# Local attention: which signals TensorE awaits before it turns the queries

## The reference

```python
h = shift_token(x)
q, k, v = jnp.split(h @ wqkv, 3, axis=-1)      # 8 heads of 64 columns
q = l2norm(q) * qs
k = l2norm(k) * ksc
q, k = rotary_xpos(q, k)
o = local_attention(q, k, v)                   # windows of 64, each sees itself and the one before
x = x + o @ wo
...
h = a * jax.nn.gelu(g, approximate=False)      # feed-forward
x = x + h @ w2 + b2
```

## Time and profile before

| | us |
|---|---|
| median of 3 runs | 2104.4 (2103.34 to 2105.58) |
| time of the profiled execution | 2106.7 |
| its span, first to last instruction | 2104.9 |
| local attention, layer 0 | about 1300 to 1600 |
| feed-forward part of layer 0 | about 1600 to 1700 |
| local attention, layer 1 | about 1700 to 1980 |
| feed-forward part of layer 1 | about 1980 to 2105 |

### The profile page before, as it was taken

How to read it: one execution, slowest core, us unless ns; L and a number is a source line. 1 busy time by engine, 2 the same in 40 slices (tenths; PEclk the granted TensorE clock), 3 DMA queues, 4 the chain that set the end, 5 groups by cost and what they waited for, 6 DMA issues and landing times. The chain is left out here.

```text
span 2104.9 us, 38118 instructions
## 1 busy us (share of the span) xinstructions
PE 1719.8 (82%) x13216; PEld 959.9 (46%) x13216; DVE 1545.4 (73%) x3211; ACT 1215.5 (58%) x2673; POOL 931.1 (44%) x771
## 2 busy tenths in 40 slices
PE   5889888874899999885991575799998989999884
PEld 2333333332344444442440442566665656666553
DVE  5999999997477777751216475788885778888675
ACT  5778777762244444432444333788885368888621
POOL 5778777783002222222443133555552145555310
PEclk7999999998699999986996787999999999999897
DMA  4433343320311111101514423010000000000010
GB/s 147 123 111 107 115 125 107 106 65 16 106 26 39 41 37 42 42 20 45 147 56 130 140 84 116 11 26 18 17 17 18 19 11 22 22 17 17 19 41 23
DMA packets 107405, 125.56 MB, mean 60 GB/s; under 512 B 28804, under 2 KB 79151, under 8 KB 106224
## 3 DMA queue, kind: packets, MB, share of 16 engines
q1 hardware_dynamic: 103120, 115.07, 19.3%
q0 software_dynamic: 4096, 8.06, 1.2%
HBM read 71.60 MB, written 38.11 MB: 52 GB/s over the span
## 5 line engine op out<-in xcount | busy, mean ns | idle before, releaser
L394 POOL TENSOR_TENSOR m_bu<-m_dtu,m_brow 128x1024 f32<-128x1024 f32 x128 | 299.6, 2356 | 54.6 <-DVE m_hs L818 54.1
L818 DVE TENSOR_TENSOR_SCAN m_hs<-m_ps_da,m_bu 128x1024 f32<-128x1024 f32 x128 | 291.9, 2280 | 6.0 <-POOL m_bu L394 5.5
L1363 ACT ACTIVATE a_pt<-a_ps_s 128x1024 f32<-128x1024 f32 x128 | 131.0, 1024 | 225.6 <-PE a_ps_s L1141 225.6
L523 PE MATMUL m_ps_y_ps<-m_prod,m_ident 128*128 128x512 f32 x512 | 243.4, 598 | 0.0
L2913 ACT ACTIVATE l_pe<-l_ps_s,l_nbias,l_qs 128x128 f32<-128x128 f32 x512 | 226.4, 467 | 15.7 <-DVE l_nbias L3063 15.7
L1480 DVE TENSOR_REDUCE a_mpad<-a_ps_s 128x4 f32<-128x1024 f32 x128 | 156.8, 1225 | 91.6 <-PE a_ps_s L1133 90.5
L1133 PE MATMUL a_ps_s<-a_heads 32*128 32x256 f32 x1024 | 186.7, 444 | 43.5 <-DVE a_mpad L1480 29.0
L670 ACT ACTIVATE m_ps_da<-m_dt,m_a_neg 128x510 f32<-128x510 f32 x256 | 166.0, 681 | 73.1 <-DVE m_hs L818 72.4
L1141 PE MATMUL a_ps_s<-a_qm,a_heads 32*128 32x256 f32 x1024 | 184.3, 437 | 1.6 <-ACT a_pt L1363 1.2
L1067 POOL TENSOR_TENSOR a_rstd<-a_ve,a_mhalf 128x2 f32<-128x2 f32 x48 | 33.8, 705 | 301.5 <-DVE a_ve L1438 162.5
L828 DVE TENSOR_TENSOR m_prod<-m_hs,m_ps_c_ps 128x1024 f32<-128x1024 f32 x128 | 153.2, 1197 | 12.3 <-PE m_ps_c_ps L509 12.3
(11 more groups left out here) (344 smaller groups left out, 4210.6 us busy)
## 6 DMA issues: line engine op xcount, KB each, us to landing
m_brow<-state_rows SPq DMA_DIRECT2D x64, 512.0 KB, 4.3
slots<-m_void SPq DMA_DIRECT2D x16, 516.0 KB, 5.4
l_near<-l_v SPq DMA_DIRECT2D x64, 128.0 KB, 2.3
e_xs<-slots SPq DMA_DIRECT2D x16, 258.0 KB, 2.8
ys<-m_void SPq DMA_DIRECT2D x8, 512.0 KB, 5.4
qk<-a_qk SPq DMA_DIRECT2D x16, 256.0 KB, 2.0
a_heads<-qk SPq DMA_DIRECT2D x64, 64.0 KB
ew_w<-in_w SPq DMA_DIRECT2D x2, 2048.0 KB, 11.9
```

Source lines behind the costliest of these rows:

```text
L394: nc.gpsimd.tensor_tensor(bu[s % 4][:, :, :], dtu[p][:, :, :], b2, ALU.mult).then_inc(bu_rd, 1)
L523: last = pe.matmul(y_ps[:, h, :], ident[:, :], prod[d % 3][:, h, :], start=False, stop=(s == NS - 1))
L818: dve.tensor_tensor_scan(hs[s % 4][:, :, :].rearrange("p h t -> p (h t)"), da[s % 2][:, :, :, :].rearrange("p h q t -> p (h q t)"), bu[s % ...
L1363: nc.scalar.activation(pt[t % 2][:, :, :], s2[:, :, :], ACT.Exp).then_inc(exp_rd, 1)
```

## The change

`turn_q` keeps its wait for ScalarE's square of the projection only for chunks with i < kept[Q], the first two of a layer. For the other 30 chunks of each layer it no longer waits for it. Its other waits stay as they are, and no other instruction is added, removed or moved.

```diff
                 def turn_q(n, b, c):
                     l, i = at[n], NCH * b + c
                     pe.wait_ge(l.sum_rd[Q], i + 1)
-                    pe.wait_ge(l.sq_rd[Q], i + 1)
+                    if i < kept[Q]:
+                        pe.wait_ge(l.sq_rd[Q], i + 1)
                     at_least(pe, l.xT_sb[Q], i)
                     at_least(pe, l.pT_sb, NU * (i - 2))
                     for j in range(NP):
```

## The result

| | before | changed |
|---|---|---|
| median of the runs, us | 2103.96 (2103.34 to 2105.58, 4 runs) | 2080.03 (2079.15 to 2082.28, 4 runs) |
| ratio, 95% interval | | 0.988 (0.9868 to 0.9892) |
| profiled execution: time, span | 2106.7, 2104.9 | 2079.59, 2077.8 |

The change makes the kernel 23.9 us faster. The forecast was 26 us and 2078.5 us, with 2073 to 2088 as the range.

The account below looks back on a forecast made before the run. The bound was a closed ring from scores through maxima, exponentials, copy, `weigh` and `turn_q`, PE's list beside it, both holding the idle time. 58 x 0.43 + 0.98 + 0.35 = 26.3 us off 2104.4 gave 2078.1, rounded to 2078.5; range 2073 to 2088.

Parts of the forecast that it names:

- What `turn_q` waited for: PE's 22.8 us idle ahead of `turn_q` in 60 chunks was read as waiting for ACT's square of the queries.
- The ring: Local attention's closed chain scores, maxima, exponentials, copy, `weigh`, `turn_q`, scores: 8.96 us a turn, 8.53 after.
- The size of a step's gain: `turn_q` starting earlier in each of 58 steps was to save 0.43 us a step.
- low end: PE's idle time ahead of `turn_q`, mean 0.36 us, as the smaller gain a step; 22.2 us in all.
- like pair: `turn_k` behind the first `weigh`, 0.61 or 0.59 us after its start, taken as how closely `turn_q` would follow the second.
- The first steps: Each layer's first step, with no `weigh` ahead of `turn_q`: gains of 0.98 us in layer 0, 0.35 in layer 1.
- The sum: 58 x 0.43 + 0.98 + 0.35 = 26.3 us off the median of 2104.4 us: 2078.1, rounded to 2078.5.
- the four candidates: What might be late next: DVE, ACT, the turned keys' copy, POOL's sum; all keep room, the least 0.23 us on ACT.
- The held VectorE: Rival: DVE's long instruction returns every step, +0.66 us, leaving 7.8 us of gain: 2096.6 us; chance 0.06.
- PE's queue: Rival: after a blocking `weigh` wait, 0.17 us of gap stays ahead of `turn_q`, gain 16 us: 2088 us; chance 0.06.
- No effect: Rival: the idle time ahead of `turn_q` belongs to PE itself, so nothing changes: 2104 us; chance 0.04.
- The clock: Rival: PE without rest in the stage loses granted clock; at 0.90, 31 us slower: 2135 us; chance 0.02.

Follow-up runs that it names:

- E3: Kernel before with ACT's two squares exchanged, keys first, so the queries' square ends later; wait kept: 2170.55 us, 1.0137 of the kernel before.
- E2: Kernel before with ACT squaring the queries ahead of the copy of the turned keys, all waits kept: 2119.21 us, 0.9888 of the kernel before.
- E1: Kernel before with the wait dropped in layer 1 alone, layer 0 keeping it: 2128.2 us, 0.9937 of the kernel before.
- E5: Changed kernel with an early-satisfied wait for DVE's rotary products of the queries in place of the dropped one: 2110.43 us, 0.988 of the kernel before.
- E8: Changed kernel without the last of eight exponentials in each chunk but a layer's first: 2116.23 us, 0.9861 of the kernel before.
- E9: Changed kernel projecting only half of the values from block 1 on: 2119.4 us, 0.9873 of the kernel before.
- E7: Changed kernel with one more reduction of the key squares on DVE in each step: 2118.35 us, 0.9906 of the kernel before.
- E11: Changed kernel as it is, run again on another chip: 2082.37 us, 0.9881 of the kernel before.

## Why the prediction was right

**What `turn_q` waited for.** Right. The profile had called it "issue", and the prediction read it as ACT's square by the 0.10 us behind its end. E3 moved that end by 0.49 us and the idle time followed; E2 moved it the other way and the idle time vanished.

**The ring.** Right. The stalls added up, and none of it was given back. E1 shows it by halves and E3 as a slope: 0.49 us later in each step, 0.50 us more a step. The turn that was forecast at 8.53 us takes 8.54.

**The size of a step's gain.** Forecast 0.43 us, with 0.36 as the low end; measured 0.40 us: 29 steady steps went from 258.05 to 246.42 us in layer 0 and from 258.04 to 246.34 in layer 1, 23.3 us in all. The start of `turn_q` moved exactly as the like pair said, 0.59 and 0.61 us behind the start of `weigh`. What the term left out is what follows. Held up, `turn_q` was followed by the scores 0.99 us after its start; not held up, by 1407.04 - 1406.02 = 1.02 us, the second of its four transposes coming 0.16 instead of 0.14 us behind the first. 58 x 0.03 = 1.7 us of the 26.3 us: the term was sized too large by that.

**The first steps.** Forecast 0.98 and 0.35 us. From first to second maxima they went from 8.32 and 8.32 us to 7.36 and 7.45 us, so 0.96 and 0.87 us. The second was undersized, and part of what came was luck. VectorE's little idle time there, 0.35 us, came of its being late, and it was late because it had waited for the projections. PE and DVE in the kernel before:

```profile
1702.02 2.94 PE L2630 MATMUL l_ps_qk<-t_wqkv,l_hT 128*128 128x512 f32 x4
...
1704.13 0.69 DVE L3031 TENSOR_TENSOR l_c<-l_ps_qk,t_tab 128x512 f32<-128x512 f32 x1 [0.57 <-PE l_ps_qk L2630]
```

And the same projections in the changed kernel:

```profile
1688.11 2.49 PE L2630 MATMUL l_ps_qk<-t_wqkv,l_hT 128*128 128x512 f32 x4
```

In the steady steps the four take 1.88 us. How much of the longer time falls to them depends on when PE's clock rises there, and I had read it from one execution as if it were fixed. From 1702 to 1704 the granted clock of the kernel before was 0.51, from 1688 to 1690 that of the changed kernel 0.71. As long as `turn_q` waits for the square the length of the projections doesn't show: 8.32, 8.33 and 8.32 us with projections of 1.98, 2.50 and 2.94 us (before, layer 0; E1, layer 0; before, layer 1). Without that wait the step follows them: 7.36 us with 1.98, 7.45 with 2.49, 7.75 with 2.85 (E5, layer 0) and 7.89 with 3.05 (E8, layer 1). So with the 2.94 us of the kernel before it would have been some 7.8 us, an estimate from these rows: a gain of 0.5 us. The other 0.4 us goes with the shorter projections.

**The sum.** Steady and first steps together gave 23.3 + 0.96 + 0.87 = 25.2 us in the traces, of 26.3 forecast. The medians moved by 23.9 us, and the 1.3 us between are scatter of executions that these runs don't place. The sum came to 2078.1 us and was put on record as 2078.5; the median was 2080.03. So two misses of opposite sign, 1.6 us too much in the steps and 0.5 too little in the first ones, partly cancelled.

**The profiled execution** moved by 27.1 us where the medians moved by 23.9. 1.2 us of it lay ahead of the local attention (its first maxima at 1324.31 instead of 1325.51), which the change doesn't touch, and 0.7 us in the last step of layer 1, where the granted clock was 0.76 before and 0.87 after. That is scatter between executions.

**What is late next.** None of the four candidates ran out, as forecast, and the idle times ahead of VectorE's maxima and of ACT's first work fell to 0.33, 0.46, 0.28 and 0.53 us for 0.29, 0.44, 0.23 and 0.51 forecast. But the nearest neighbour of the ring wasn't among the four. It was PE's own list, which the prediction had seen to run beside it and not measured: 8.48 us against 8.50. It didn't take from the gain, because the idle time stood in it too, as the prediction had said. It does take from any cut that shortens the ring alone, as in E8.

**The rivals.** The held VectorE: `scale_k` kept its 0.68 us but for the first step of layer 0, where it took 1.34 us again with POOL's rotary sum beside it. The keys' sum stayed at 0.69 us; in 5 of its 64 runs that rotary sum was still running beside it, for 0.2 us at most, and it took 0.77 us at most. PE's queue: no gap stayed, and E5 puts 60 satisfied waits at nothing. That rival spoke of a `weigh` that had truly blocked, and E9 has one: it is held for 0.37 us and starts at 1435.97, and `turn_q` follows at 1436.56, 0.59 us behind it. No effect: ruled out by E2 and E3. The clock: 1.00 in the stage, with PE busy for 59.63 of 60 us.

## What to carry to other kernels

Idle time that a profile ascribes to "issue" ahead of an instruction with several waits is worth a look at what ended just before it on the other engines; moving that one producer, earlier or later, shows whether the wait is for it. A stall inside a closed ring of engines was worth its whole length in every turn here, up to the point at which the next chain is as long, and two chains of like length have to be cut together: each alone gave 0 to 0.02 us a step here, both together 0.43. For the size of a gain or of a room take the distance from start to start of a like pair that nothing holds up, and for all that follows too, not the idle time.

## What the runs showed that I had not expected

- Idle times understate room. VectorE's mean 0.39 us a step was 0.50 us in E7, and PE's 0.36 us ahead of `turn_q` was worth 0.40, as shown durations run past the start of an instruction that isn't held.
- The group of four transposes in `turn_q` takes 0.03 us longer from its start to that of what follows when it comes right behind other work than when PE had been idle ahead of it.
- The kernel before took 2104 to 2146 us from one set of runs to the next, each set on another chip, while two steps without the late wait took 16.99 to 17.02 us in each of them (E2, E5, E9 and E11). Much of the difference lies ahead of this stage: its first maxima stand at 1324 to 1328 us in the traces of the two faster sets and at 1354 to 1372 us in those of the three slower ones.
